# Expert tile 2 issued in quarters inside the second score block

## The chip, the cores and the metric

The kernel runs on one core of one Trainium2 chip. The metric is the device time of one execution in microseconds (us); lower is better. The kernel before has a median of 1390.96 us over three runs (1388.37 to 1396.16).

## The reference

Two layers, each an attention and a feed-forward part, with a residual sum and a layer norm behind each part. The input is 8 batches of 1024 tokens of 256 features; the batches do not depend on each other. Cut to what the change touches:

```python
# layer 0, feed-forward: 8 experts, soft gate with a threshold
gate_logits = softmax(x @ gate_w + gate_b)
weights = gate_logits * (gate_logits >= 0.1);  weights /= sum(weights)
for e in range(8):
    out = out + weights[:, e:e+1] * (x @ expert_w[e] + expert_b[e])
...
# layer 1, attention: per token, among its 16 heads of 16 features
q, k, v = split(einsum('bnm,fm->bnf', x, Wqkv).reshape(b, n, 16, 48))
scores = einsum('bnhd,bngd->bnhg', q, k) / 8
out = einsum('bnhg,bngd->bnhd', softmax(scores), v)
out = out.reshape(b, n, 256) @ Wproj.T + bproj
```

The attention of layer 1 is between the 16 heads of one token, so its products are small. Layer 0's attention is a linear one over features, and layer 1's feed-forward part works on the three quarters of the tokens that a router picks; neither is touched.

## The kernel before, in words

**Stages and turns.** The program has three stages per batch: a (layer 0's attention), b (layer 0's experts and the q, k, v projection of layer 1) and c (the rest of layer 1). A turn works on batch i in stage a, batch i-1 in stage b and batch i-2 in stage c. Each engine has a function `turn(a, b, c)` that writes out its order by hand, and the engines meet through semaphores alone. An engine works its list strictly from top to bottom. With 8 batches there are seven turns that hold both b and c, and these are the turns that the change touches.

**Expert tiles.** A batch has eight token tiles of 128. For tile t, TensorE's `a_moe` (line 1699) makes four quarters q, each six products 128x512 into PSUM bank 4 + q (two experts a quarter; every number is split into two fp16 parts, hence three products for each half of the features). A product of this kind is called wide. Quarter q may start when the same quarter of tile t-1 has been read. VectorE (`a_moe`, line 1252) reads quarters 0 and 1 and adds four experts to the tile. ScalarE (`a_moe`, line 834) evicts quarters 2 and 3, scaled, into four parts of the buffer `part`, two evictions a quarter; before tile t's first it waits for `moe_ready` of tile t-1, since GpSimd's `a_sum` (line 547) has to have summed that tile's `part` and added it.

**Score blocks.** The scores are made in four blocks q. `b_s` on TensorE (line 1725) issues 96 products 128x16 (called narrow) for a block: four groups of 24, each for one residue of the token. Blocks use PSUM banks 2 and 3 in turn, with the transposed probabilities between: block 0 in bank 2, block 1 in bank 3, transposes 0 in bank 2, block 2 in bank 3, transposes 1 in bank 2, block 3 in bank 3. Then for each block: VectorE's `b_s` (line 1303) takes the maximum and subtracts, ScalarE's `b_s` (line 769) takes the exponential, VectorE's `b_ssum` (line 1312) sums and inverts, GpSimd's `b_s` (line 594) multiplies, and TensorE's `b_pt` (line 1739) transposes. ScalarE's `b_pt` (line 774) and VectorE's (line 1319) then write the high and low half of the transposed block into the buffer `ct`. That buffer holds the loaded V until GpSimd has copied it away in two halves (`b_turnv`, line 582), so `b_pt` waits for both copies.

**The order around the change, in a turn with b and c.** TensorE: expert tile 1, score blocks 0 and 1, tile 2, transposes 0, block 2, transposes 1, block 3, tile 3, transposes 2 and 3, output blocks. VectorE: tile 1, block 0 and its sum, block 1 and its sum, tile 2, the statistics of the first pair, low half of transposes 0, block 2. ScalarE: evictions of tile 1, exponentials 0 and 1, evictions of tile 2, high half of transposes 0. GpSimd: sum of tile 0, first half of V, sum of tile 1, probabilities 0 and 1, second half of V, sum of tile 2, a layer norm, probabilities 2 and 3.

Of the kernel before, what the change touches and what calls it, by code (L numbers as in the profile page):

```python
# [5 lines left out]
def build_two_layer_postln(nc, x, wqk_t, bqk, wv, bv, gamma, gate_w, gate_b, expert_w, expert_b,  # L6
# [37 lines left out]
    with ctx:  # L44
# [3 lines left out]
        def sem(name):  # L48
            return ctx.enter_context(nc.semaphore(name))
# [113 lines left out]
        b_full = sem("b_full")  # L163
# [76 lines left out]
        def a_ring(name):  # L240
            return a_use(name) % 2

        def b_ring(name):
            return b_use(name) % 2
# [4 lines left out]
        def b_filled(b, name):  # L249
            return b * UB + b_use(name) + 1  # L250

        def a_read(a, name):
            return a * (UA // 2) + a_use(name) // 2 + 2

        def b_read(b, name):
            return b * (UB // 2) + b_use(name) // 2 + 2
# [5 lines left out]
        def b_before(b, name):  # L262
            return b_read(b, name) - 1
# [10 lines left out]
        def later(n):  # L274

            return not (isinstance(n, int) and n == 0)
# [4 lines left out]
        def b_ps(name):  # L281
            return b_bank[b_use(name) % 2][:, :]
# [413 lines left out]
        def _(act):  # L696
# [72 lines left out]
            def b_s(b, q):  # L769
                act.wait_ge(b_free[b_ring(f"S{q}")], b_read(b, f"S{q}"))  # L770
                act.activation(prob[:, q % 2, :], prob[:, q % 2, :], ACT.Exp, scale=ATT_SCALE)\
                    .then_inc(p_exp, 1)
# [61 lines left out]
            def a_moe(a, t):  # L834
                act.wait_ge(wt_ready, a + 1)
                if t == 0 and later(a):
                    act.wait_ge(*f_stored(a - 1, 3))
                for q in (2, 3):
                    act.wait_ge(m_full, 32 * a + 4 * t + q + 1)
                    if q == 2 and t >= 1:  # L840
                        act.wait_ge(moe_ready, T * a + t)
                    for h in range(2):
                        ins = copy(part[:, 2 * (q - 2) + h, :], m_bank[q][:, D * h:D * (h + 1)],
                                   wexp[:, t, 2 * q + h:2 * q + h + 1])
                    ins.then_inc(m_free[q], 1)
                act.wait_ge(m_free[3], T * a + t + 2)
                act.sem_inc(parted, 1)  # L847
# [38 lines left out]
            def b_turnv(b, hf):  # L886
                act.wait_ge(v_loaded, 16 * T * (b + 1))
                copy(v_rows[hf].rearrange("p (s c) h -> p s c h", c=8),
                     compact[:, :, 8 * hf:8 * hf + 8, :]).then_inc(v_turned[hf], 1)
# [11 lines left out]
            def turn(a, b, c):  # L901
# [15 lines left out]
                    a_moe(b, 1)  # L917
                if c is not None:
                    b_s(c, 0)
                    b_s(c, 1)  # L920
                if b is not None:
                    a_moe(b, 2)
                elif c is not None:
                    b_turnv(c, 0)
                if c is not None:
                    b_pt(c, 0)
# [149 lines left out]
            for p in range(TP):  # L1076
                a_xs(0, p)
            turn(0, None, None)
            turn(1, 0, None)
            for i in range(2, NB):  # L1080
                turn(i, i - 1, i - 2)
# [5 lines left out]
        def _(dve):  # L1087
# [164 lines left out]
            def a_moe(a, t):  # L1252
                dst = x1[:, t, :]
                if t % 2 == 0:
                    dve.wait_ge(a_free[a_ring(f"BIAS{t // 2}")], a_read(a, f"BIAS{t // 2}"))
                for e in range(4):
                    q = e // 2
                    if e % 2 == 0:
                        dve.wait_ge(m_full, 32 * a + 4 * t + q + 1)
                    ins = dve.scalar_tensor_tensor(out=dst, in0=m_bank[q][:, D * (e % 2):D * (e % 2 + 1)],  # L1260
                                                   scalar=wexp[:, t, e:e + 1], in1=dst, op0=ALU.mult,
                                                   op1=ALU.add)
                    if e % 2 == 0:
                        ins.then_inc(m_step, 1)
                        dve.wait_ge(m_step, 2 * T * a + 2 * t + q + 1)
                    else:
                        ins.then_inc(m_free[q], 1)
                        if q == 0:
                            dve.wait_ge(m_free[q], T * a + t + 2)
                dve.wait_ge(m_free[1], T * a + t + 2)  # L1270
                dve.sem_inc(chained, 1)

            def a_ln2(a, p):
                dve.wait_ge(moe_ready, T * a + 2 * p + 2)
                pair_stats([x1[:, 2 * p + t, :] for t in range(2)], a, 4 + p, 0)
# [27 lines left out]
            def b_s(b, q):  # L1303
                dve.wait_ge(b_full, b_filled(b, f"S{q}"))
                ps = b_ps(f"S{q}").rearrange("p (a g) -> p a g", g=H)
                pr = prob[:, q % 2, :].rearrange("p (a g) -> p a g", g=H)
                dve.tensor_reduce(smax[:, :], ps, X, ALU.max).then_inc(v_step_b, 1)
                dve.wait_ge(v_step_b, done_b.next(b))
                dve.tensor_tensor(pr, ps, smax[:, :, None].broadcast_to([P, 32, H]),
                                          ALU.subtract).then_inc(b_free[b_ring(f"S{q}")], 1)  # L1310

            def b_ssum(b, q):
                pr = prob[:, q % 2, :].rearrange("p (a g) -> p a g", g=H)
                dve.wait_ge(p_exp, 4 * b + q + 1)
                dve.tensor_reduce(ssum[:, :], pr, X, ALU.add).then_inc(v_step_b, 1)
                dve.wait_ge(v_step_b, done_b.next(b))
                dve.reciprocal(srec[:, q % 2, :], ssum[:, :]).then_inc(p_rec, 1)
# [73 lines left out]
            def turn(a, b, c):  # L1391
# [7 lines left out]
                if c is not None:  # L1399
                    b_s(c, 0)  # L1400
                    b_ssum(c, 0)
                    b_s(c, 1)
                    b_ssum(c, 1)
                if b is not None:
                    a_moe(b, 2)
                    a_ln2(b, 0)
                if c is not None:
                    b_pt(c, 0)
# [148 lines left out]

            dve.wait_ge(w_first, 16 * N_FIRST)
            turn(0, None, None)
            turn(1, 0, None)  # L1560
            for i in range(2, NB):
                turn(i, i - 1, i - 2)
# [6 lines left out]
        def _(pe):  # L1569
            def sum_of(dst, terms):  # L1570

                for n, (lhs, rhs) in enumerate(terms):
                    ins = pe.matmul(dst, lhs, rhs, start=(n == 0), stop=(n == len(terms) - 1))  # L1573
                return ins

            def split_terms(lhs, rhs):

                return [(lhs(k, i), rhs(k, j)) for k in range(KD) for i, j in PASSES]
# [8 lines left out]
            def tok(t):  # L1587
                return slice(P * t, P * (t + 1))
# [110 lines left out]
            def a_moe(a, t, qs=range(4)):  # L1699
                for q in qs:  # L1700
                    if t == 0 and later(a):
                        pe.wait_ge(ff_read, 4 * (a - 1) + q + 1)
                    pe.wait_ge(m_free[q], T * a + t + 1)
                    sum_of(m_bank[q][:, :], split_terms(lambda k, i: at[:, k, i, tok(t)],
                                                        lambda k, j: we[:, j, k, 512 * q:512 * (q + 1)]))\
                        .then_inc(m_full, 1)
# [14 lines left out]
            def block(q, part, t, c):  # L1721

                return blockdiag[:, q // 2, 64 * part + 8 * t + 4 * (q % 2) + c, :]

            def b_s(b, q):
                if q == 0:
                    pe.wait_ge(k_loaded, 16 * T * (b + 1))
                pe.wait_ge(q_spread[q // 2], (1 + q // 2) * (b + 1))
                pe.wait_ge(b_free[b_ring(f"S{q}")], b_before(b, f"S{q}"))
                for c in range(4):  # L1730
                    for g in range(T):
                        token = 16 * g + 4 * q + c
                        n = T * c + g
                        ins = sum_of(b_ps(f"S{q}")[:, H * n:H * (n + 1)],
                                     [(block(q, i, g, c), keys[:, :, P * j + token])
                                      for i, j in PASSES])
                ins.then_inc(b_full, 1)

            def b_pt(b, q):
                pe.wait_ge(p_ready, 4 * b + q + 1)  # L1740
# [69 lines left out]
            def turn(a, b, c):  # L1810
# [4 lines left out]
                    a_moe(b, 1)  # L1815
                if c is not None:
                    b_s(c, 0)
                    b_s(c, 1)
                if b is not None:
                    a_moe(b, 2)  # L1820
                if c is not None:
                    b_pt(c, 0)
                    b_s(c, 2)
                    b_pt(c, 1)
                    b_s(c, 3)
# [127 lines left out]
            for i in range(2, NB):  # L1953
                turn(i, i - 1, i - 2)
# [52 lines left out]
```

## Time and profile before

| | us |
|---|---|
| median of three runs | 1390.96 |
| lowest and highest | 1388.37, 1396.16 |
| the profiled execution | 1388.98 |
| its span, first to last instruction | 1387.0 |

| engine | busy us | share of the span |
|---|---|---|
| TensorE, products | 1175.5 | 85% |
| VectorE | 925.7 | 67% |
| ScalarE | 732.5 | 53% |
| GpSimd | 578.7 | 42% |

The mean granted clock of TensorE was 0.879 of full speed. The profile names engines PE (TensorE), DVE (VectorE), ACT (ScalarE) and POOL (GpSimd). The busy share is a mean over stages with different limits; what a change in one stage does is read from that stage's chain of waits. A product's line is mostly that of the helper that issues it (`sum_of`, line 1573), so that products are told apart by the names behind it: `we,at` are the experts' products, `keys,blockdiag` the scores', `const,prob` the transposes of probabilities.

### The profile page before, as it was taken

To read this page: it belongs to the slowest core of one execution; us is meant where nothing else is said; L and a number is where in the kernel's file an instruction comes from. 1 tells how busy PE (TensorE), PEld (TensorE's weight loads), DVE (VectorE), ACT (ScalarE), POOL (GpSimd) and SP (SyncE) were. 2 spreads that over 40 slices of the span, in tenths; PEclk is the share of its full clock that TensorE was granted. 3 is DMA by queue.
4 is the path that set the end of the run, shared out by engine and by line. 5 is a ranking of instruction groups with operands and counts; after the bars stand their busy time and mean duration, and the time that the engine had idled before them with its cause. 6 is when DMAs were issued, how large, how long until landed. Compare 5 with 4: busy or idle time off the path is not lost.

```text
span 1387.0 us, 31167 instructions
## 1 busy us (share of the span) xinstructions
PE 1175.5 (85%) x12264; PEld 751.8 (54%) x12264; DVE 925.7 (67%) x2113; ACT 732.5 (53%) x1156; POOL 578.7 (42%) x887
## 2 busy tenths in 40 slices
PE   6688898998989899998989899998989888775643
PEld 3444456655655556655665556655665546542542
DVE  3544677587766878587776877577766877465624
ACT  3222475346654685347653685347654685355623
POOL 3135335425535545425525535425525525333212
PEclk8689998899979998899979997899969998798566
DMA  5000091205611191206611191205610091207220
GB/s 183 15 1 16 31 158 13 78 14 128 88 32 47 47 173 13 77 16 137 78 32 47 47 173 11 78 10 126 94 31 33 31 172 13 62 1 188 26 62 31
DMA packets 93145, 90.64 MB, mean 65 GB/s; under 512 B 7110, under 2 KB 81864, under 8 KB 92744
## 3 DMA queue, kind: packets, MB, share of 16 engines
q1 hardware_dynamic: 79560, 75.02, 28.3%
q0 software_dynamic: 2560, 8.39, 1.7%
q10 hardware_dynamic: 10880, 5.25, 1.5%
q8 instruction: 98, 1.61, 0.5%
q14 instruction: 47, 0.39, 0.1%
HBM read 46.68 MB, written 41.94 MB: 64 GB/s over the span
## 4 chain that ended last, share of the span: by engine, by line
PE 40%; DVE 20%; POOL 12%; ACT 9%; issue 8%; DMA 7%; SPq 2%; ACTq 1%; POOLq 0%; DVEq 0%
PE bank L1573 37%; POOL stage L585 4%; DMA ct<-scratch_qkv 3%; DVE keys L1355 3%; SPq L458 2%; POOL rs L535 2%; DVE x L1260 2%; DVE stats L1119 2%; DVE gelu L1357 2%; DMA bt<-scratch_o 2%; ACT shared L698 2%; DVE ct L1089 1%; DMA scratch_o<-stage 1%; PE bank L1583 1%; ACT x L821 1%
## 5 line engine op out<-in xcount | busy, mean ns | idle before, releaser
L1573 PE MATMUL bank<-we,at 128*128 128x512 f16 x1536 | 370.6, 400 | 1.9 <-DVE x L1260 1.9
L1573 PEld LDWEIGHTS bank<-we,at 128*128 128x128 f16 x1536 | 153.8, 102 | 192.1 <-issue 37.6
L550 POOL TENSOR_TENSOR part<-part 128x512 f32<-128x512 f32 x64 | 84.1, 1313 | 279.9 <-ACTq L847 279.9
L698 ACT ACTIVATE part<-bank,wexp 128x256 f32<-128x256 f32 x256 | 104.8, 473 | 160.9 <-PE bank L1573 103.0
L1573 PE MATMUL bank<-bt,wqkv 128*128 128x512 f16 x576 | 138.9, 383 | 23.4 <-DVE stage L1089 17.0
L821 ACT ACTIVATE x<-x,nm,rs 128x256 f32<-128x256 f32 x192 | 105.1, 596 | 100.0 <-POOL nm L538 98.7
L1260 DVE SCALAR_TENSOR_TENSOR x<-bank,wexp,x 128x256 f32<-128x256 f32 x256 | 122.8, 480 | 49.8 <-PE bank L1573 43.2
L531 POOL TENSOR_SCALAR nm<-mv 128x2 f32<-128x2 f32 x128 | 34.9, 272 | 253.8 <-DVE mv L1124 248.3
L1089 DVE TENSOR_TENSOR stage<-bank,stage 128x512 f16<-128x512 f32 x112 | 75.6, 686 | 89.1 <-ACT stage L698 88.9
L1573 PE MATMUL bank<-keys,blockdiag 128*128 128x16 f16 x3072 | 97.0, 193 | 20.1 <-DVE blockdiag L1287 9.7
L698 ACT ACTIVATE stage<-bank 128x512 f16<-128x512 f32 x112 | 66.1, 597 | 82.7 <-PE bank L1573 77.0
L1573 PEld LDWEIGHTS bank<-keys,blockdiag 128*128 128x128 f16 x3072 | 95.5, 104 | 25.2 <-issue 23.7
L1573 PEld LDWEIGHTS bank<-bt,wqkv 128*128 128x128 f16 x576 | 52.5, 98 | 91.2 <-DVE stage L1089 27.8
L1573 PE MATMUL bank<-ct,blockdiag 128*128 128x16 f16 x3072 | 83.4, 173 | 19.6 <-issue 19.6
L535 POOL TENSOR_TENSOR rs<-ve,half 128x2 f32<-128x2 f32 x128 | 94.4, 737 | 10.7
L1573 PEld LDWEIGHTS bank<-ct,blockdiag 128*128 128x128 f16 x3072 | 82.3, 102 | 22.0 <-issue 22.0
L1583 PE MATMUL bank<-const,x 128*128 128x128 f32 x384 | 60.0, 285 | 40.3 <-ACT x L821 21.7
L1089 DVE TENSOR_TENSOR ct<-bank,ct 128x512 f16<-128x512 f32 x64 | 41.6, 678 | 60.8 <-ACT ct L698 60.8
L585 POOL COPY stage<-ct 128x2048 f16<-128x2048 f16 x15 | 56.9, 3794 | 54.7 <-DMA ct<-scratch_qkv 54.7
L698 ACT ACTIVATE blockdiag<-stage,const 128x2048 f16<-128x2048 f16 x40 | 78.2, 1995 | 0.0
L1119 DVE BATCH_NORM_STATS2 stats<-x 128x6 f32<-128x256 f32 x192 | 71.9, 417 | 8.2 <-POOL x L557 4.1
L1583 PEld LDWEIGHTS bank<-const,x 128*128 128x128 f32 x384 | 45.5, 145 | 56.0 <-ACT x L821 28.7
(181 smaller groups left out, 2253.8 us busy)
## 6 DMA issues: line engine op xcount, KB each, us to landing
scratch_qkv<-stage SPq DMA_DIRECT2D x40, 512.0 KB, 3.3
ct<-scratch_qkv SPq DMA_DIRECT2D x120, 128.0 KB, 6.8
x_in<-in_x_dram SPq DMA_DIRECT2D x32, 256.0 KB, 2.7
keys<-scratch_qkv SPq DMA_DIRECT2D x64, 128.0 KB, 5.8
bt<-scratch_o SPq DMA_DIRECT2D x16, 512.0 KB, 3.8
out_dram<-x POOLq DMA_DIRECT2D x32, 256.0 KB, 2.6
scratch_qkv<-part SPq DMA_DIRECT2D x8, 512.0 KB, 8.4
scratch_o<-stage SPq DMA_DIRECT2D x32, 128.0 KB, 3.4
```

The lines of the kernel that those rows point to most:

```text
L531: pool.tensor_scalar(nm[side][:, k, :], mv[side][:, k, :, 0], -1.0, None, ALU.mult)
L535: pool.tensor_tensor(rs[side][:, k, :], ve[side][:, k, :], half[:, 0:2], ALU.pow)\
L550: pool.tensor_tensor(part[:, 0:2, :], part[:, 0:2, :], part[:, 2:4, :], ALU.add)\
L585: pool.tensor_copy(v_rows[hf].rearrange("p (s c) h -> p s c h", c=8), compact[:, :, 8 * hf:8 * hf + 8, :]).then_inc(v_turned[hf], 1)
L698: return act.activation(dst, src, ACT.Copy, scale=scale)
L821: ins = act.activation(dsts[t], srcs[t], ACT.Identity, bias=nm[side][:, k, t:t + 1], scale=rs[side][:, k, t:t + 1])
L1089: return dve.tensor_tensor(dst, src, hi, ALU.subtract)
L1119: ins = dve.bn_stats(stats[side][:, t, :], srcs[t])
L1260: ins = dve.scalar_tensor_tensor(out=dst, in0=m_bank[q][:, D * (e % 2):D * (e % 2 + 1)], scalar=wexp[:, t, e:e + 1], in1=dst, op0=ALU.mult ...
L1355: dve.tensor_scalar(beats_on[:, o:o + P * (T - 1 - t)], scores[:, P * (t + 1):C], me, None, ALU.is_le, ALU.add, accum_out=rowsum[:, t, 0:1])
L1573: ins = pe.matmul(dst, lhs, rhs, start=(n == 0), stop=(n == len(terms) - 1))
L1583: ins = pe.transpose(ps[:, 2 * P * k + P * t:2 * P * k + P * (t + 1)], src[:, 2 * p + t, P * k:P * (k + 1)], ident)
```

## The change

In a turn with b and c, TensorE issues expert tile 2 in quarters inside score block 1: behind each 24 narrow products of the block come the six wide ones of one quarter. The block's signal goes out behind its last narrow product, ahead of the last quarter. VectorE reads tile 2 ahead of block 1 instead of behind it, and ScalarE evicts tile 2 ahead of the exponential of block 1 instead of behind it. Tiles 1 and 3 keep their places. GpSimd's and SyncE's lists are as before.

```diff
@@ ScalarE, turn
                 if c is not None:
                     b_s(c, 0)
+                if b is not None:
+                    a_moe(b, 2)
+                if c is not None:
                     b_s(c, 1)
-                if b is not None:
-                    a_moe(b, 2)
-                elif c is not None:
+                if b is None and c is not None:
                     b_turnv(c, 0)
@@ VectorE, turn
                 if c is not None:
                     b_s(c, 0)
                     b_ssum(c, 0)
+                if b is not None:
+                    a_moe(b, 2)
+                if c is not None:
                     b_s(c, 1)
                     b_ssum(c, 1)
                 if b is not None:
-                    a_moe(b, 2)
                     a_ln2(b, 0)
@@ TensorE, b_s
-            def b_s(b, q):
+            def b_s(b, q, tile=None):
...
                         ins = sum_of(b_ps(f"S{q}")[:, H * n:H * (n + 1)],
                                      [(block(q, i, g, c), keys[:, :, P * j + token])
                                       for i, j in PASSES])
-                ins.then_inc(b_full, 1)
+                    if c == 3:
+                        ins.then_inc(b_full, 1)
+                    if tile is not None:
+                        a_moe(b + 1, tile, (c,))
@@ TensorE, turn
                 if c is not None:
                     b_s(c, 0)
-                    b_s(c, 1)
-                if b is not None:
+                    b_s(c, 1, None if b is None else 2)
+                elif b is not None:
                     a_moe(b, 2)
```

TensorE, from tile 1's last quarter to block 2, in the first turn that has all three stages, before and then with the change (bank 3 is block 1, banks 4 to 7 are the quarters of the tile):

```order
L1573 MATMUL bank7<-we,at 128x512 x6
L1573 MATMUL bank2<-keys,blockdiag 128x16 x96
L1573 MATMUL bank3<-keys,blockdiag 128x16 x96
L1573 MATMUL bank4<-we,at 128x512 x6
L1573 MATMUL bank5<-we,at 128x512 x6
L1573 MATMUL bank6<-we,at 128x512 x6
L1573 MATMUL bank7<-we,at 128x512 x6
L1743 MATMUL bank2<-const,prob 128x128 x4
```

```order
L1576 MATMUL bank7<-we,at 128x512 x6
L1576 MATMUL bank2<-keys,blockdiag 128x16 x96
L1576 MATMUL bank3<-keys,blockdiag 128x16 x24
L1576 MATMUL bank4<-we,at 128x512 x6
L1576 MATMUL bank3<-keys,blockdiag 128x16 x24
L1576 MATMUL bank5<-we,at 128x512 x6
L1576 MATMUL bank3<-keys,blockdiag 128x16 x24
L1576 MATMUL bank6<-we,at 128x512 x6
L1576 MATMUL bank3<-keys,blockdiag 128x16 x24
L1576 MATMUL bank7<-we,at 128x512 x6
L1750 MATMUL bank2<-const,prob 128x128 x4
```

The number of products is the same; block 1's last 24 now stand behind three quarters of tile 2.

ScalarE in the same place, before and then with the change (`part` is written by the evictions of a tile, `prob<-prob` is an exponential, `ct<-bank` the high half of transposed probabilities):

```order
L698 ACTIVATE part<-bank,wexp 128x256 x4
L771 ACTIVATE prob<-prob 128x512 x2
L698 ACTIVATE part<-bank,wexp 128x256 x4
L698 ACTIVATE ct<-bank 128x512
L771 ACTIVATE prob<-prob 128x512
```

```order
L698 ACTIVATE part<-bank,wexp 128x256 x4
L771 ACTIVATE prob<-prob 128x512
L698 ACTIVATE part<-bank,wexp 128x256 x4
L771 ACTIVATE prob<-prob 128x512
L698 ACTIVATE ct<-bank 128x512
L771 ACTIVATE prob<-prob 128x512
```

The four evictions of tile 2 have moved from behind the exponential of block 1 to ahead of it.

## Rows read from the trace of the kernel before

**Rows 1.** The page: TensorE's busy time, and the chain that ended last by engine.

```profile
PE 1175.5 (85%) x12264; PEld 751.8 (54%) x12264; DVE 925.7 (67%) x2113; ACT 732.5 (53%) x1156; POOL 578.7 (42%) x887
PE 40%; DVE 20%; POOL 12%; ACT 9%; issue 8%; DMA 7%; SPq 2%; ACTq 1%; POOLq 0%; DVEq 0%
```

**Rows 2.** Chain of waits, first turn: start us, length us, what.

```profile
219.68 2.07 POOL prob L597 x2
221.76 3.78 POOL stage L585
...
225.64 0.61 ACT ct L698
...
226.27 0.69 DVE ct L1089
226.96 0.61 DVE smax L1307
...
227.59 0.70 DVE prob L1309
...
228.43 9.86 PE bank L1573 x120
```

**Rows 3.** Timeline of TensorE, first turn: start, length, operation, count, [idle before].

```profile
204.43 5.34 PE L1573 MATMUL bank<-we,at 128*128 128x512 f16 x24
209.61 6.08 PE L1573 MATMUL bank<-keys,blockdiag 128*128 128x16 f16 x192
215.53 6.38 PE L1573 MATMUL bank<-we,at 128*128 128x512 f16 x24
...
231.26 7.04 PE L1573 MATMUL bank<-we,at 128*128 128x512 f16 x24
```

**Rows 4.** Timelines of ScalarE and of VectorE, first turn, block 1 and tile 2.

```profile
217.80 0.63 ACT L771 ACTIVATE prob<-prob 128x512 f32<-128x512 f32 x1 [2.41 <-DVE prob L1309]
...
221.94 0.84 ACT L698 ACTIVATE part<-bank,wexp 128x256 f32<-128x256 f32 x2 [0.41 <-PE bank L1573]
...
218.46 0.69 DVE L1315 TENSOR_REDUCE ssum<-prob 128x32 f32<-128x512 f32 x1 [0.70 <-ACT prob L771]
219.18 0.35 DVE L1317 RECIPROCAL srec<-ssum 128x32 f32<-128x32 f32 x1
```

**Rows 5.** Third turn: TensorE's blocks 0 and 1 (timeline), GpSimd in the chain.

```profile
522.03 6.05 PE L1573 MATMUL bank<-keys,blockdiag 128*128 128x16 f16 x192
...
531.49 0.53 POOL prob L597
...
533.52 3.76 POOL stage L585
```

**Rows 6.** Seventh turn: the same.

```profile
1144.52 6.04 PE L1573 MATMUL bank<-keys,blockdiag 128*128 128x16 f16 x192 [2.22 <-issue]
...
1155.50 2.07 POOL prob L597 x2
1157.58 3.74 POOL stage L585
```

**Rows 7.** Fourth turn: TensorE's tile 2, VectorE's low half and its maximum of block 2.

```profile
683.79 7.75 PE L1573 MATMUL bank<-we,at 128*128 128x512 f16 x24
...
693.40 0.69 DVE L1089 TENSOR_TENSOR ct<-bank,ct 128x512 f16<-128x512 f32 x1 [1.98 <-ACT ct L698]
694.87 0.69 DVE L1307 TENSOR_REDUCE smax<-bank 128x32 f32<-128x512 f32 x1 [0.78 <-PE bank L1573]
```

**Rows 8.** Stretches: PE, PEld, DVE, ACT, POOL busy us, then granted clock, DMA.

```profile
213.00:214.00 1.00, 1.00 (x39) 1.00 (x36) 0.85 (x2) 0.00 (x0) 0.91 (x1) 1.00 0.00 0
215.00:216.00 1.00, 1.00 (x25) 0.72 (x22) 0.58 (x1) 0.39 (x1) 1.00 (x1) 0.50 0.00 0
1149.50:1152.90 3.40, 3.40 (x41) 1.74 (x38) 2.63 (x5) 0.63 (x1) 3.40 (x2) 0.50 0.00 0
1152.95:1156.70 3.75, 3.75 (x19) 1.72 (x18) 2.95 (x6) 1.47 (x3) 3.59 (x5) 1.00 0.00 0
```

More of the change, by code:

```diff
@@ L919, in turn @@
                     b_s(c, 0)
-                    b_s(c, 1)
                 if b is not None:
                     a_moe(b, 2)
-                elif c is not None:
+                if c is not None:
+                    b_s(c, 1)
+                if b is None and c is not None:
                     b_turnv(c, 0)
@@ L1817, in turn @@
                     b_s(c, 0)
-                    b_s(c, 1)
-                if b is not None:
+                    b_s(c, 1, None if b is None else 2)
+                elif b is not None:
                     a_moe(b, 2)
```

## The prediction

> **What bounds the kernel now.** I read the page first, then the chain of waits in the seven turns that hold both expert tiles and score blocks, then the timelines of the engines on it, and last the granted clock. The page [rows 1] gives TensorE 85% of the span and 40% of the chain that ended last. An average cannot tell whether TensorE binds at the place that is edited, so that place is read by itself. In the first of the seven turns the chain there [rows 2] is not on TensorE: GpSimd multiplies the probabilities of score blocks 0 and 1 (219.68, 2.07 us for the two), copies the second half of V (221.76), and only then may ScalarE write the transposed probabilities over the compact buffer (225.64); VectorE takes their low half (226.27), reads score block 2 (226.96 and 227.59), and TensorE gets bank 3 for block 3 at 228.43. TensorE [rows 3] had finished tile 2 at 215.53 + 6.38 = 221.91 and block 2 soon after, and stood waiting. The second copy of V is on the chain in six of the seven turns; the third and the seventh are shown [rows 5, 6]. In the fourth turn TensorE was last instead [rows 7]: VectorE ended the low half at 693.40 + 0.69 = 694.09 and began on block 2 at 694.87, so GpSimd's path had 0.78 us to spare.
>
> **What the change moves.** No product, copy or DMA is added or dropped, beyond the wait and the signal that each quarter already had. Three orders change, in seven turns; GpSimd's, SyncE's and the DMA queues' do not.
>
> TensorE. Before, block 0 and block 1 ran as 192 narrow products in 215.53 - 209.61 = 5.92 us, 2.96 us a block, and 24 wide ones at full clock took 209.61 - 204.43 = 5.18 us [rows 3]. From the start s of block 0, the mixed stretch is then done at s + 2.96 + 2.96 + 5.18 = s + 11.10, and block 1 is complete a quarter of tile 2 earlier, at s + 11.10 - 1.30 = s + 9.80; before it was s + 5.92. Tile 2's third quarter ends before the last 24 narrow ones (0.74 us), at s + 9.06. Against the 12.30 us that TensorE took before (221.91 - 209.61), that is 1.2 us less for TensorE. The changeovers between narrow and wide I cost at nothing: the wide row of tile 1 ends at 209.77 by its length, and the narrow row behind it starts at 209.61 [rows 3], so no gap shows; the cover is TensorE's own queue, and a price of up to 0.16 us each, seven in a block, stays in the range.
>
> ScalarE. This is the dear part. Before, the exponential of block 1 stood ahead of the four evictions of tile 2; now it stands behind them. The first two evictions need tile 2's third quarter, and the buffer `part`, which GpSimd has summed for tile 1 only when it turns to the probabilities, at 219.68 = s + 10.07 in the first turn [rows 2]. The last two need the fourth quarter, s + 11.10; two evictions take 0.84 us [rows 4]. So the last pair starts at the later of s + 11.10 and GpSimd's time plus 0.84, which is s + 11.10 in the first turn. Behind it come 0.84 of eviction, 0.63 of exponential [rows 4], 0.69 and 0.35 of VectorE's sum and reciprocal [rows 4], and 1.04 of GpSimd's product (half of 2.07), with some 0.03 us at each of three handovers (218.46 - 217.80 - 0.63): 3.65 us. GpSimd, whose order is fixed, stands idle for this and can start the second copy of V at s + 11.10 + 3.65 = s + 14.75. Before it was 221.76 - 209.61 = s + 12.15.
>
> VectorE. Its four steps of tile 2 now stand ahead of block 1. They find quarter 1 done by s + 7.0 (2.96 and twice 0.74 and 1.30), take some 1 us each quarter and are over before block 1 is complete, so they cost nothing; were block 1 done sooner they would. Block 1 then takes 1.4 us and is read at s + 11.2, before ScalarE is free at s + 11.94: nothing either.
>
> **The sum.** First turn: 14.75 - 12.15 = 2.60 us later. Third [rows 5]: block 0 starts at 522.03, GpSimd is done with the tile at 531.49, the copy began at 533.52, s + 11.49; the same working gives s + 14.75, 3.26 us later. Seventh [rows 6]: block 0 at 1144.52, GpSimd at 1155.50 (s + 10.98, so that the last pair starts at s + 11.82), the copy at 1157.58 (s + 13.06) against s + 15.47: 2.41 us later. Their mean is 2.76 us; six turns make 16.5 us. The fourth turn has 0.78 us of slack first: 2.0 us. Together 18.5 us. I take it as passed on whole: everything behind the copy on every engine (low half, block 2, block 3, tile 3, the output blocks) waits in order on it, the chain runs from 228.43 through block 3 and tile 3 without a break [rows 2], and the next turn's V load starts from products that stand behind them all.
>
> **The clock.** The price of wide products depends on it. Narrow products alone lose it: at 213 to 214 us TensorE was busy 1.00 and had 2.4 GHz, at 215 to 216 us it was busy 1.00 and had 0.50 of that, 1.2 GHz [rows 8]. That made tile 2 take 6.38 us [rows 3] and in the fourth turn 7.75 us [rows 7] where 5.34 is the row at full clock: 1.04 to 2.41 us. In the new order the longest narrow run is 120 products (block 0 and the first quarter of block 1) instead of 192. Such a run can lose the clock, or not. The bounds are no turn of seven and all seven at 2.41, that is 0 to 17 us. I take two turns at 1.5 us, 3 us, nearer the low end: a single block of 96 in the middle of wide work is half of the old run and 120 is a quarter of the way from 96 to 192; and only some of the wide products fall into a slow stretch, since a mixed stretch at 0.50 with 41 products (1149.50 to 1152.90) was followed by one at 1.00 [rows 8].
> The Trainium skill (TensorE: Matmul & The Clock Gate, section Why this matters for your kernels) has it that TensorE gets and keeps the full clock by being kept busy, and drops when it idles. By that rule the mixed stretch would never slow and the sum would be 18.5 us; by the row, busy 1.00 beside 0.50, it is 21.5. Here the measurement decides.
>
> The profiled execution took 1388.98 us (span 1387.0): 1388.98 + 18.5 + 3 = 1410.5. The median of the three runs is 1390.96, 2 us above it, so I say **1412 us**.
>
> **The rivals.**
> (a) TensorE sets the end there after all, and the change is faster. Then what counts is when tile 2 is done: 6.38 or 7.75 us shrink to 5.18, 1.2 to 2.6 us a turn, some 1.9 on average, 13 us over seven turns: 1378. It decides only where V's second copy is over about 3 us before VectorE needs it; one turn of seven had even 0.78 us [rows 7]. For it speaks the 85% on the page. Chance 0.06.
> The Trainium skill (Perfetto Trace Analysis, sections Identifying the Most-Contended Engine and Optimization Strategy) says to optimize the busiest engine first and that interleaving regimes with different limits may help; this rival is that rule, and the chain of six turns disagrees with it here.
> (b) The delay is made but given back: tile 3 took 7.04 us at 231.26 [rows 3], 1.70 over the row at full clock. Should tile 3 find the full clock in each turn, 7 x 1.70 = 11.9 of the 18.5 us come back: about 1398, within the noise. Against it: TensorE now waits longer ahead of block 3, and in that wait it does nothing that would raise the clock. Chance 0.08.
> (c) The mixed stretch stays at 1.2 GHz to its end. Then 24 wide products take twice 5.18 us, 5.2 us more per turn, all of it ahead of the last eviction: 7 x 5.2 = 36, on top of 18.5: 1446. Against it: the stretch at 1149.50 of narrow and wide products got the full clock back [rows 8]. Chance 0.06.
>
> **How the numbers follow.** The forecast has 0.80. Its own range: low, seven turns at the fourth's 2.0 us and no loss of clock, 14 us, 1405; high, seven at the largest 3.26 (22.8) and 1.5 us of clock in all seven (10.5), 33 us, 1424. To hold 8 in 10 it is widened toward (b): 1400 to 1427. A measurement of this kernel tells some 0.5%, 7 us, from no change. Faster by more than that is (a), 0.06. Within it is (b) and a little of the forecast's low edge, 0.10. Slower is the rest, 0.84.
>
> **What would show it.** Right: in the chain, ahead of V's second copy, ScalarE's evictions of tile 2 and the exponential of block 1 stand where GpSimd's pair of products stood; the pair is split by some 3 us of idle GpSimd; V's second copy starts 14.5 to 16.5 us after block 0; TensorE waits more than 4 us ahead of block 3; and tile 2's last quarter still ends about 11 to 12.5 us after block 0, earlier than before. Wrong: V's second copy at the old 12 us, or a shift there that is not found again at the first output block, or a granted clock of 0.50 through the mixed stretch.

## The result, and the profile after

| | before | with the change |
|---|---|---|
| median, us | 1392.56 (4 runs) | 1415.49 (4 runs, 1412.08 to 1420.96) |
| ratio to before, 95% interval | | 1.0169 (1.0122 to 1.0217) |
| profiled execution, its span, us | 1388.98, 1387.0 | 1412.08, 1410.0 |

The change makes the kernel 1.7% slower; 1412 was forecast. The page of the changed kernel, its engines' busy time and its chain by engine, against [rows 1]:

```profile
PE 1170.2 (83%) x12264; PEld 750.7 (53%) x12264; DVE 925.1 (66%) x2113; ACT 730.9 (52%) x1156; POOL 577.7 (41%) x887
PE 38%; DVE 19%; POOL 12%; ACT 10%; issue 9%; DMA 8%; SPq 3%; ACTq 1%; POOLq 0%; DVEq 0%
```

TensorE is busy 5.3 us less and the span is 23 us longer: what TensorE saved, it now waits. The chain of waits of the changed kernel (start, length, what), in the first turn, which answers to [rows 2], and at the same place in the third and the seventh turn:

```profile
218.52 1.02 POOL prob L597
219.53 3.35 issue
...
222.92 1.06 POOL prob L597
223.97 3.57 POOL stage L585
...
227.65 0.61 ACT ct L698
...
230.44 10.13 PE bank L1576 x120
...
535.02 4.86 issue
...
540.98 3.57 POOL stage L585
...
1174.75 2.57 issue
...
1178.42 3.57 POOL stage L585
```

GpSimd's products of blocks 0 and 1, one piece before, are split by 3.35 us in which GpSimd does nothing (4.86 and 2.57 in the others). V's second copy starts 15.10, 15.11 and 16.73 us after block 0 in these three turns, where it was 12.15, 11.49 and 13.06 [rows 2, 3, 5, 6]. TensorE's timeline of the changed kernel, first turn, and the start of block 0 in the third and the seventh, against [rows 3, 5, 6]:

```profile
208.87 3.86 PE L1576 MATMUL bank<-keys,blockdiag 128*128 128x16 f16 x120
212.57 1.46 PE L1576 MATMUL bank<-we,at 128*128 128x512 f16 x6
...
218.65 1.46 PE L1576 MATMUL bank<-we,at 128*128 128x512 f16 x6
...
229.11 1.09 PE L1750 MATMUL bank<-const,prob 128*128 128x128 f32 x4 [5.68 <-DVE ct L1090]
230.44 2.99 PE L1576 MATMUL bank<-keys,blockdiag 128*128 128x16 f16 x96 [0.24 <-DVE prob L1310]
...
525.87 3.86 PE L1576 MATMUL bank<-keys,blockdiag 128*128 128x16 f16 x120
...
1161.69 3.84 PE L1576 MATMUL bank<-keys,blockdiag 128*128 128x16 f16 x120 [2.21 <-issue]
```

Tile 2 is done at 220.11, 11.24 us after block 0, where it took 12.30 before; the gain goes into the wait of 5.68 us ahead of transposes 1. ScalarE in the same turn, against [rows 4]: the exponential of block 1 now stands behind both pairs of evictions.

```profile
218.63 0.84 ACT L698 ACTIVATE part<-bank,wexp 128x256 f32<-128x256 f32 x2 [3.98 <-POOL x L557]
220.15 0.84 ACT L698 ACTIVATE part<-bank,wexp 128x256 f32<-128x256 f32 x2 [0.67 <-PE bank L1576]
221.10 0.63 ACT L771 ACTIVATE prob<-prob 128x512 f32<-128x512 f32 x1
```

The seven turns, in us from the start of block 0, read from TensorE's timelines of both kernels:

| turn | tile 2 ends, before | after | block 3 starts, before | after | later by |
|---|---|---|---|---|---|
| 1 | 12.3 | 11.2 | 18.8 | 21.6 | 2.8 |
| 2 | 12.3 | 11.2 | 18.8 | 21.6 | 2.8 |
| 3 | 13.1 | 11.2 | 18.2 | 21.6 | 3.4 |
| 4 | 15.0 | 12.5 | 19.9 | 22.8 | 2.9 |
| 5 | 12.9 | 12.5 | 19.4 | 23.0 | 3.6 |
| 6 | 12.8 | 11.2 | 18.6 | 21.6 | 3.0 |
| 7 | 12.4 | 12.7 | 19.7 | 23.2 | 3.5 |

Before rounding, the last column sums to 21.9 us. From block 3 to the end of tile 3 the seven turns take 70.4 us together instead of 69.1. That makes 23.2 us, and the span grew by 23.0: all the rest of the program differs by 0.2 us in sum. So close a sum is partly luck: over the traces of all kernels here, block 0 of the first of these turns starts anywhere from 206.87 to 211.73 us, though no edit touches what stands ahead of it. The first output blocks start 23.5 us later in sum, so the delay is passed on.

### The profile page after: what moved, and what is told of

The parts are those of the page before. It is cut to its first block, busy times and chain, and to the rows that moved or that the text cites. A ratio compares the mean times of both kernels' runs of the same rounds, so it can differ in the third digit from the quotient of the medians.

```text
span 1410.0 us, 31167 instructions
## 1 busy us (share of the span) xinstructions
PE 1170.2 (83%) x12264; PEld 750.7 (53%) x12264; DVE 925.1 (66%) x2113; ACT 730.9 (52%) x1156; POOL 577.7 (41%) x887
## 4 chain that ended last, share of the span: by engine, by line
PE 38%; DVE 19%; POOL 12%; ACT 10%; issue 9%; DMA 8%; SPq 3%; ACTq 1%; POOLq 0%; DVEq 0%
PE bank L1576 35%; DMA ct<-scratch_qkv 4%; POOL stage L585 4%; SPq L458 3%; DVE keys L1356 3%; DVE x L1261 2%; DVE stats L1120 2%; ACT shared L698 2%; POOL rs L535 2%; DVE gelu L1358 2%; DMA bt<-scratch_o 2%; DVE ct L1090 1%; PE bank L1586 1%; DMA scratch_o<-stage 1%; ACT x L821 1%
## 5 line engine op out<-in xcount | busy, mean ns | idle before, releaser
L1576 PEld LDWEIGHTS bank<-we,at 128*128 128x128 f16 x1536 | 150.9, 101 | 182.1 <-issue 28.8
L1576 PE MATMUL bank<-bt,wqkv 128*128 128x512 f16 x576 | 139.1, 383 | 22.6 <-DVE stage L1090 16.8
L1576 PE MATMUL bank<-keys,blockdiag 128*128 128x16 f16 x3072 | 100.0, 193 | 14.3 <-issue 12.4
L1576 PEld LDWEIGHTS bank<-ct,blockdiag 128*128 128x128 f16 x3072 | 82.5, 102 | 22.0 <-issue 21.9
```

## The experiments

The theory: GpSimd makes V's second copy behind block 1's product, so whatever delays block 1's softmax delays the copy, and block 3 with it. The rivals: ScalarE's order alone; the mixed stretch or its clock on TensorE; a place elsewhere in the turn. In the diffs, c is the batch in stage c.

### Only TensorE's part, and only ScalarE's and VectorE's

`e1_tensor_only` is the changed kernel with these lists as before:

```diff
@@ ScalarE, turn
                 if c is not None:
                     b_s(c, 0)
+                    b_s(c, 1)
                 if b is not None:
                     a_moe(b, 2)
-                if c is not None:
-                    b_s(c, 1)
-                if b is None and c is not None:
+                elif c is not None:
                     b_turnv(c, 0)
@@ VectorE, turn
                     b_s(c, 0)
                     b_ssum(c, 0)
-                if b is not None:
-                    a_moe(b, 2)
-                if c is not None:
                     b_s(c, 1)
                     b_ssum(c, 1)
                 if b is not None:
+                    a_moe(b, 2)
                     a_ln2(b, 0)
```

> TensorE keeps the mixed stretch; ScalarE and VectorE get their old order back (exponential of block 1 ahead of the evictions of tile 2). Theory (block 1's softmax is late for GpSimd, and GpSimd makes V's second copy only behind it): block 1 is still complete only some 10.0 us after block 0 starts, so the copy starts at 14.2 us after block 0, against 15.1 in the changed kernel and 12.1 before: about 6 us faster than the changed kernel, 1409 us, still 1.2% slower than before. Rival 1 (ScalarE's new order alone makes the loss): back to the kernel before, 1392 us. Rival 2 (the mixed stretch itself is slow on TensorE): no gain, 1415 us.

Measured: 1403.43 us, ratio 1.0093 (1.0057 to 1.0129). TensorE's block 0 in the first turn, and the chain there:

```profile
206.87 3.85 PE L1573 MATMUL bank<-keys,blockdiag 128*128 128x16 f16 x120
...
218.30 1.02 POOL prob L597
219.31 0.76 issue
...
220.11 1.06 POOL prob L597
221.17 3.72 POOL stage L585
```

The copy starts 14.30 us after block 0, close to the 14.2 worked out; 15.10 in the changed kernel, 12.15 before. So TensorE's later block 1 alone makes 2.1 us of the delay, and ScalarE's order adds 0.8 on top. Rival 1 falls, since a loss of 0.9% stays without ScalarE's order; rival 2 falls, since the slowest of the four runs (1408.35) is faster than the fastest of the changed kernel (1412.08). The time is some 11 us under the changed kernel's by the two ratios, and not 6: block 3 starts 6.9 us earlier over the seven turns, and from there to the end of tile 3 it takes 67.0 us against 70.4. What rival (b) of the prediction thought of, tile 3 with more of the full clock, happens here in part.

`e2_scalar_only` is the kernel before with ScalarE's and VectorE's lists of the change.

> TensorE gets its old order back (block 1, then tile 2); ScalarE and VectorE keep the new one (tile 2 ahead of block 1). Theory: the exponential of block 1 now waits for the end of tile 2, which in the kernel before is 12.3 to 15.0 us after block 0, and 3.9 us later the copy starts, at 16 to 19 us: some 30 us slower than before, 1423 us, slower than the changed kernel too. Rival 1 (ScalarE's order alone makes the loss of the change): as the changed kernel, 1415 us. Rival 2 (the mixed stretch makes the loss): as before, 1392 us.

Measured: 1419.97 us, ratio 1.0216 (1.0181 to 1.0252). The edit is the diff of the change above without its two parts on TensorE. TensorE's timeline in the second turn, and the chain there:

```profile
372.01 6.06 PE L1576 MATMUL bank<-keys,blockdiag 128*128 128x16 f16 x192
377.92 6.50 PE L1576 MATMUL bank<-we,at 128*128 128x512 f16 x24
```

```profile
383.88 3.32 issue
...
387.23 1.06 POOL prob L597
388.29 3.57 POOL stage L585
```

Tile 2 ends at 384.42, the copy starts 3.87 us behind it, 16.28 us after block 0. In the traces ScalarE's order costs more without the mixed stretch than with it, since the end of tile 2 is then later: block 3 starts some 30 us later than before over the seven turns, and 21.9 with the whole change. The times alone do not separate the two kernels, as their intervals overlap. The two parts of the change do not add: block 1's softmax, and the copy behind it, wait for the later of two things, block 1's completion and tile 2's last eviction.

### V's second copy off that path

`e3_v_before_block1` moves one line of the changed kernel, on GpSimd:

```diff
                     b_s(c, 0)
+                    b_turnv(c, 1)
                     b_s(c, 1)
-                    b_turnv(c, 1)
```

> The changed kernel with one line moved on GpSimd: V's second copy stands ahead of block 1's product instead of behind it. Theory (the loss is nothing but this copy waiting behind the late softmax of block 1): the copy starts at 11.1 us after block 0, when block 0's product is done, block 3 starts at some 17.8 us instead of 22.2 (before: 19.0), 7 x 4.4 = 31 us less than the changed kernel: 1385 us, under the kernel before. Rival (block 1's late softmax holds block 3 by itself, through transposes 1): block 3 gains less than 2 us and the time stays above 1400 us.

Measured: 1385.28 us, ratio 0.9954 (0.9933 to 0.9975). GpSimd's timeline, second turn:

```profile
375.35 1.06 POOL L597 TENSOR_TENSOR prob<-prob,srec 128x512 f32<-128x512 f32 x1
376.36 3.88 POOL L585 COPY stage<-ct 128x2048 f16<-128x2048 f16 x1
380.20 1.05 POOL L597 TENSOR_TENSOR prob<-prob,srec 128x512 f32<-128x512 f32 x1
```

Block 0's product, the copy and block 1's product stand without a gap, and block 3 starts 17.8 to 19.9 us after block 0. One line on GpSimd turns 1.7% slower into 0.5% faster, with the change's orders on TensorE, ScalarE and VectorE in place. So the loss sat in the copy's wait. That the copy's place may be worth something without the change too is what the next pair tests.

`e4_v_on_scalar` takes the copy from GpSimd in the seven turns of the changed kernel, and `e5_before_v_on_scalar` does so in the kernel before. The edit of `e4_v_on_scalar`:

```diff
@@ GpSimd, turn
                     b_s(c, 0)
                     b_s(c, 1)
+                if c is not None and b is None:
                     b_turnv(c, 1)
@@ ScalarE, turn
                 if c is not None:
                     b_s(c, 0)
+                if b is not None and c is not None:
+                    b_turnv(c, 1)
                 if b is not None:
                     a_moe(b, 2)
```

In `e5_before_v_on_scalar` ScalarE's line stands in the same place, behind `b_s(c, 0)`, and there `b_s(c, 1)` follows it.

> The changed kernel, but ScalarE instead of GpSimd makes V's second copy in the seven turns, behind the exponential of block 0, where it waits for tile 2 anyway. Theory: the late softmax of block 1 no longer holds the copy, block 3 starts 17.3 us after block 0 (18.5 where the clock is lost) against 22.2 in the changed kernel and 19.0 before: 1383 us (1375 to 1392), faster than before. Rival 2 (the mixed stretch or its clock makes the loss): the loss stays, above 1405 us. Rival 3 (the loss is elsewhere in the turn): above 1400 us.

> The kernel before, with the same copy moved to ScalarE between the exponentials of blocks 0 and 1. Theory: TensorE's tile 2 becomes the last to be waited for there, block 3 starts some 5.1 us behind the end of tile 2, that is 17.4 to 20.1 us after block 0 against 18.2 to 19.9: 1386 us (1380 to 1393), a little slower than the changed order with the copy moved. Rival (TensorE bound already before, the copy no matter): 1392 us.

Measured: 1382.20 us, ratio 0.9932 (0.9903 to 0.9961), for the changed order, and 1380.84, ratio 0.9935 (0.9898 to 0.9972), for the old one. The first is as expected. The second lies 5 us under the figure expected, at the low end of its range. The two cannot be told apart: with the copy off GpSimd the change costs nothing that can be measured, where with the copy there it cost 1.7%. It gains nothing that can be measured either. In the traces block 3 starts 17.9 us after block 0 on average in `e4_v_on_scalar` and 18.5 in `e5_before_v_on_scalar`, 4 us over seven turns, which is about half the width of the intervals. TensorE's block 2 and the chain of `e4_v_on_scalar`, second turn, show what holds block 3 back there:

```profile
379.10 3.02 PE L1579 MATMUL bank<-keys,blockdiag 128*128 128x16 f16 x96
...
378.81 0.85 ACT part L699 x2
...
379.76 0.64 ACT prob L772
...
380.43 0.70 DVE ssum L1319
...
381.42 0.70 DVE stats L1123 x2
...
382.50 0.57 DVE ct L1093
383.08 0.61 DVE smax L1311
```

TensorE's block 2 had ended at 379.10 + 3.02 = 382.12, yet VectorE reads it at 383.08: behind the late sum of block 1 and the statistics of another tile, which stand ahead of the low half in its list. Part of the delay of block 1 has moved from GpSimd to VectorE.

### A shorter run of narrow products

`e9_shorter_narrow_run` places the four quarters of the changed kernel behind the third group of block 0 and the first, second and fourth of block 1. The longest narrow run is then 72.

```diff
+            AFTER = {(0, 2): 0, (1, 0): 1, (1, 1): 2, (1, 3): 3}
...
-                    if tile is not None:
-                        a_moe(b + 1, tile, (c,))
+                    if tile is not None and (q, c) in AFTER:
+                        a_moe(b + 1, tile, (AFTER[q, c],))
...
-                    b_s(c, 0)
+                    b_s(c, 0, None if b is None else 2)
                     b_s(c, 1, None if b is None else 2)
```

> The changed kernel, but the first quarter of tile 2 goes ahead of block 0's last 24 narrow products, so that the longest run of narrow products is 72 and not 120; block 1 is complete, and tile 2 done, at the same 9.8 and 11.1 us after block 0 starts. Theory (the clock is lost in three of seven turns because the 120 narrow ones stand together): the granted clock stays at 1.00 through the stretch in all seven turns, tile 2 ends at 11.2 us and V's second copy starts at 15.05 us in each, 4 us less than the changed kernel, 1411 us. Rival (the loss comes from what lies ahead of block 0, whatever the order in it): three of seven turns still end tile 2 at 12.5 us; 1415 us.

Measured: 1416.87 us, ratio 1.0182 (1.0146 to 1.0219): no gain. The 4 us expected are less than such an interval can show, so the theory is tested by the trace, which is that of the slowest of the four runs (1421.86). The clock did what was expected where nothing else came between: in the fourth and fifth turns, which lost it in the changed kernel, it was 1.00 throughout, and tile 2 ended at 11.6 us in five of seven turns. In the seventh TensorE stands idle for 2.2 us ahead of block 0 in both kernels and loses the clock either way. In the third something else happened. The stretch of the fourth turn, then TensorE in the third, then VectorE in the third and the fourth:

```profile
692.40:704.00 11.60, 11.41 (x219) 8.49 (x218) 8.84 (x17) 3.10 (x8) 7.49 (x5) 1.00 0.17 18
...
528.84 2.37 PE L1576 MATMUL bank<-keys,blockdiag 128*128 128x16 f16 x72
534.87 2.74 PE L1576 MATMUL bank<-we,at 128*128 128x512 f16 x6 [3.67 <-DVE x L1261]
...
527.71 6.19 DVE L1288 TENSOR_SCALAR blockdiag<-shared,const 128x2048 f16<-128x2048 f16 x4
...
691.25 2.73 DVE L1288 TENSOR_SCALAR blockdiag<-shared,const 128x2048 f16<-128x2048 f16 x4
```

Tile 2's first quarter needs its bank read by VectorE for tile 1, and VectorE was late: its four spreads (masked copies of q into the scores' operand) took 6.19 us there, 2.73 in the fourth turn. Behind the wait of 3.67 us the quarter took 2.74 us instead of 1.46, so the clock was lost as well. The new order asks for that bank earlier: in the five good turns TensorE waits 0.2 us for it. But it did not make VectorE late; by its start at 528.84 and 3.70 us for 120 narrow products, the old order would still have waited some 2.3 us there, an estimate. So the theory on the clock is borne out in the turns without a long wait, and no time was gained.

### A version that beats both

`e6_v_scalar_stats_later` joins V's copy on ScalarE, the shorter narrow run, and VectorE's statistics (`a_ln2(b, 0)`) moved from ahead of the low half of transposes 0 to behind block 2's difference. `e7_sum_before_v` adds GpSimd's sum of tile 1 (`a_sum(b, 1)`) ahead of V's first copy (`b_turnv(c, 0)`).

> The kernel with V's second copy on ScalarE, with the shorter narrow run, and with VectorE's statistics of the first pair moved from ahead of the low half of transposes 0 to behind block 2's maximum and difference. Theory: VectorE's chain loses 1.0 us and the clock loss of up to 1.3 us goes, so that block 3 starts 16.2 us after block 0 instead of 17.0 to 18.9, except where V is loaded late: about 1372 us, 1.5% under the kernel before. Rival (what follows, the spreads of V and block 3, sets the output blocks): block 3 starts earlier but the first output block does not, 1382 us.

> The same, and GpSimd sums tile 1 ahead of V's first copy instead of behind it. Theory: in the turns where V is loaded 5.6 us after block 0 starts instead of 3.4, ScalarE's evictions of tile 2 wait for that sum; ahead of the copy it is done by 6.5 us, and block 3 starts 16.2 us after block 0 in all seven turns: 1369 us. Rival (in those turns the wait for V itself sets block 3, by the first copy): no gain over the kernel it builds on.

Measured: 1375.01 us, ratio 0.9874 (0.9839 to 0.9908), and 1374.42, ratio 0.9875 (0.9847 to 0.9904). Both beat the kernel before by 1.3%, some 3 and 5 us less than expected. TensorE of the second kernel, second turn:

```profile
363.58 2.37 PE L1581 MATMUL bank<-keys,blockdiag 128*128 128x16 f16 x72
...
380.11 3.01 PE L1581 MATMUL bank<-keys,blockdiag 128*128 128x16 f16 x96
```

Block 3 starts 16.5 us after block 0 in six of seven turns in both (16.8 in one of the first kernel). What each of the three parts of `e6_v_scalar_stats_later` brings was not tried one by one. In the seventh turn, 19.6 and 19.1, TensorE idles 2.2 us ahead of block 0, waits another 1.2 us for VectorE inside the stretch, and makes the first quarter at the low clock (2.74 us). GpSimd's sum is not what holds it, and the second step brought nothing that can be measured.

`e10_best_unmixed` is the second kernel with the old order of tile 2 and block 1 on TensorE, ScalarE and VectorE.

> The fastest kernel so far with TensorE's, ScalarE's and VectorE's old order of tile 2 and block 1: V's second copy on ScalarE, the statistics behind block 2, GpSimd's sum of tile 1 ahead of V's first copy. It tells what the mixed stretch is worth where V's copy binds no longer. Theory: block 3 starts 4.9 us behind tile 2's end, and that is 12.2 to 14.7 us after block 0 since the 192 narrow products lose the clock: block 3 at 17.1 to 19.6 us, mean 18, against 16.5 to 19.1 with the mixed stretch: 1381 us, some 0.5% over the mixed one. Rival (the mixed stretch is worth nothing): 1374 us.

Measured: 1382.29 us, ratio 0.9938 (0.9915 to 0.9961), 0.6% over the mixed one, and the intervals do not meet. Its chain in the second turn, where block 0 starts at 365.33:

```profile
359.99 17.80 PE bank L1579 x252
377.79 0.44 PE bank L1749 x4
378.22 2.87 PE bank L1579 x96
...
381.12 0.70 DVE smax L1310
```

Here TensorE is on the chain from block 0 to block 2, so that tile 2's time counts, and the mixed stretch pays: with it block 3 starts 5.6 us earlier over the seven turns, and the way from there to the end of tile 3 is shorter by another 3.8.

## Why the prediction was right

**What bounds.** Right. The chain of six turns lay on GpSimd's second copy. One moved line (`e3_v_before_block1`) took the whole loss away, and with the copy on ScalarE the old and the new order take the same time (`e4_v_on_scalar`, `e5_before_v_on_scalar`).

**TensorE's part.** Right in size: s + 11.10 for the end of tile 2 was 11.24 by the profile. No price showed for the changeovers: block 0, the first quarter and the next narrow products start at 208.87, 212.57 and 213.87, that is 3.70 us for 120 narrow products, as at the pace of [rows 3], and 1.30 for a quarter.

**ScalarE's part.** The instant was right within 0.35 us: 15.10 instead of 14.75, since the last pair began at 220.15 (11.28) and the way from there to the copy took 3.82 us and not 3.65. Some of it came back, as the copy itself took 3.57 us instead of 3.78. But "the dear part" was wrongly shared out. By `e1_tensor_only` TensorE's later block 1 gives 2.1 us with ScalarE's list untouched; ScalarE's move adds 0.8 on top. The prediction worked out only what both give together. Its signs came: V's second copy started 15.1 us after block 0 in four turns, and 16.3 to 16.7 in the three that lost the clock, where 16.5 was its upper bound.

**The sum.** 18.5 us for the seven turns without the clock: 21.9 less the 3.9 that the clock took (below) is 18.0. With the clock it is 21.5 against 21.9. The 1.3 us more between block 3 and the end of tile 3 were put at nothing.

**The clock.** Two turns at 1.5 us were taken, three were found, at 1.2, 1.3 and 1.4 (by the ends of tile 2, 12.48, 12.49 and 12.68 us against 11.24). The bounds named were far apart, 0 to 17 us, so a figure this near is partly luck. The changed kernel's stretches (engines' busy us, then the granted clock), first turn and fourth:

```profile
212.00:220.00 8.00, 8.00 (x121) 5.20 (x118) 5.72 (x11) 1.47 (x3) 7.38 (x5) 1.00 0.00 0
684.80:687.80 3.00, 3.00 (x101) 3.00 (x100) 2.90 (x6) 1.60 (x5) 0.00 (x0) 1.00 0.62 60
687.90:691.20 3.30, 3.30 (x37) 1.63 (x34) 2.42 (x4) 0.63 (x1) 2.76 (x1) 0.50 0.02 5
```

In the fourth turn TensorE was busy 3.00 of 3.00 us with narrow products at 2.4 GHz and then had 1.2 GHz for the first quarter, as in [rows 8]. With the narrow run cut to 72 (`e9_shorter_narrow_run`) that turn and the fifth kept 1.00. The seventh has 2.21 us of idle time ahead of block 0 and is another case.

The Trainium skill (TensorE: Matmul & The Clock Gate, section Why this matters for your kernels) has TensorE get the full clock by being kept busy and lose it in idle gaps between products. The fourth turn does not agree with this, busy 3.00 of 3.00 us and yet slowed. In the seventh there is idle time, but a narrow run follows it, and no run here separates the two.

**The rivals.** (a), TensorE at the end, did not come about: tile 2 ended earlier and block 3 later. It became true only once the copy was on ScalarE and VectorE's statistics stood later, 0.6% by `e10_best_unmixed` against `e7_sum_before_v`. (b), tile 3 at full clock, did not: 70.4 us against 69.1. (c), the mixed stretch at 1.2 GHz to its end, did not: the granted clock was 1.00 in four turns, and two quarters at most were slow in the others.

The Trainium skill (Perfetto Trace Analysis, section Optimization Strategy) says that interleaving regimes with different most-contended engines may improve the time. In the pair of `e7_sum_before_v` and `e10_best_unmixed` it did, by 0.6%; in the change as it was made it cost 1.7%.

## What to carry to other kernels

When work is put between the parts of a step, ask what stands behind that step in the order of every engine that takes part, also of those whose list is not edited: here a copy that had nothing to do with block 1 stood behind its product on GpSimd. An interleaving that saves time on the busiest engine is worth that time only after the chain at that place runs through this engine; move the stranger out of the way first, then measure the interleaving with and without. Two delays that meet in one wait do not add, so undo them one at a time before saying which is dear.

## What the runs showed of the hardware

Where a copy on GpSimd and a spread on VectorE, both of fp16, met, the one that came second took longer. The first two rows are from `e9_shorter_narrow_run`, the last two from the changed kernel, third turn in both:

```profile
529.58 3.75 POOL L585 COPY stage<-ct 128x2048 f16<-128x2048 f16 x1 [5.00 <-DMA ct<-scratch_qkv]
529.69 4.20 DVE L1288 TENSOR_SCALAR blockdiag<-shared,const 128x2048 f16<-128x2048 f16 x1
...
526.23 4.91 POOL L585 COPY stage<-ct 128x2048 f16<-128x2048 f16 x1 [4.62 <-DMA ct<-scratch_qkv]
526.73 0.74 DVE L1288 TENSOR_SCALAR blockdiag<-shared,const 128x2048 f16<-128x2048 f16 x1
```

Of the four spreads that took 6.19 us, three took 0.74 each. The last began 0.11 us behind the start of GpSimd's copy, took 4.20 us and ended 0.56 behind the copy's end. In the changed kernel the copy began while spreads were running: they kept their 0.74 us, and the copy took 4.91 us, ending 3.67 behind the last of them. So it looks as if the one that came second stood until the other was through. That is an inference from these two meetings; it was not tried by itself.

A long run of narrow products is enough to lose the full clock, with TensorE busy throughout, but not always. Counted over the stretch from block 0 to the end of tile 2 in the traces: with 192 in a row (`before`, `e2_scalar_only`, `e5_before_v_on_scalar`, `e10_best_unmixed`) the granted clock fell in all 28 turns, idle time in them or not. With 120 (`after`, `e1_tensor_only`, `e3_v_before_block1`, `e4_v_on_scalar`) it fell in 7 of the 24 first to sixth turns, in one of them behind a wait of 0.39 us. With 72 (`e9_shorter_narrow_run`, `e6_v_scalar_stats_later`, `e7_sum_before_v`) it fell in one of 18, behind the wait of 3.67 us. In the seventh turn of these last seven kernels TensorE idled 0.5 to 2.2 us ahead of block 0, and the clock fell in each.
